# Raw tiles of x landing in the resident array, modulation weights early, loads of two tiles, even shares per step

## The reference, cut to what matters

```python
x = L0_attn_x                                   # (1, 8192, 512)
mod = (_silu(L0_c) @ L0_wmod).reshape(1, 6, 1, 512)
sa, ca, ga, sb, cb, gb = ...                    # ga, gb: magnitude at least 0.25
h = _layernorm(x) * (1 + ca) + sa
x = x + ga * ssm_block(h)     # scan over 8192 steps, 16x16 matrix per channel; layernorm, gelu, W_out, +h
h = _layernorm(x) * (1 + cb) + sb
x = x + gb * ffn_block(h)     # Win, 64 small relu networks of 16, Wout
```

## Time and profile before

| what | us |
|---|---|
| median of 3 runs (lowest, highest) | 761.77 (761.5, 762.27) |
| profiled execution, span of the core from first to last instruction (the only time shown for it) | 763.1 |
| first matmul of the power stage | 10.54 |
| last statistics of x on DVE end | 93.34 |
| last normalised tile on ACT ends | 102.81 |
| first matmul behind the stage (L1185) | 105.20 |

### The profile page before, as it was taken

The page is one execution under the profiler, slowest core; times in us unless marked ns, Lnnn a source line. Parts: engine busy times, 40 slices in busy tenths (PEclk is TensorE's granted clock), DMA queues, the critical chain, the costliest instruction groups (busy, mean ns, idle before and its releaser), DMA issues.

```text
span 763.1 us, 24715 instructions
## 1 busy us (share of the span) xinstructions
PE 706.2 (93%) x10079; PEld 493.9 (65%) x10079; DVE 533.1 (70%) x1192; ACT 470.9 (62%) x1007; POOL 483.1 (63%) x684
## 2 busy tenths in 40 slices
PE   5797978899999898999699999999999999999997
PEld 4774867888899877887545555555455555555564
DVE  7886866844643468544734688788888888877776
ACT  1674966133322471244246888888988888888872
POOL 5664633743455507654288988788888888887710
PEclk9999999999999999999889999999999999999999
DMA  7977400259500002388423002322232232231114
GB/s 223 364 229 274 154 17 3 44 122 174 127 6 4 3 24 45 86 200 177 143 92 111 1 30 82 111 105 81 92 111 83 85 110 84 84 111 55 57 41 153
DMA packets 78209, 78.18 MB, mean 102 GB/s; under 512 B 16144, under 2 KB 49552, under 8 KB 78096
## 3 DMA queue, kind: packets, MB, share of 16 engines
q1 hardware_dynamic: 77072, 74.76, 32.6%
q10 hardware_dynamic: 1024, 1.84, 0.9%
HBM read 59.28 MB, written 17.30 MB: 100 GB/s over the span
## 4 chain that ended last, share of the span: by engine, by line
PE 49%; DVE 1%; POOL 0%; ACT 0%; DVEq 0%; issue 0%; ACTq 0%; POOLq 0%
PE PS L1309 30%; PE PS L1378 4%; PE PS L1356 4%; PE PS L1301 4%; PE PS L1343 4%; PE PS L1393 1%; PE PS L1319 1%; PE PS L1330 0%; ACT arenaC L664 0%; DVE ebs L979 0%; PE PS L1323 0%; DVE arenaC L995 0%; DVEq L86 0%; POOL sy L392 0%; DVE XY L833 0%
## 5 line engine op out<-in xcount | busy, mean ns | idle before, releaser
L1309 PE MATMUL PS<-arenaC,arenaA 128*128 128x512 f32 x512 | 242.0, 605 | 0.0
L408 POOL TENSOR_TENSOR arenaC<-arenaA,par 128x512 f32<-128x512 f32 x104 | 107.3, 1039 | 82.6 <-ACT arenaA L647 41.8
L1309 PEld LDWEIGHTS PS<-arenaC,arenaA 128*128 128x128 f32 x512 | 90.2, 191 | 87.6 <-issue 83.1
L1172 PE MATMUL PS<-arenaA,arenaC 64*64 64x80 f32 (+1 forms) x1792 | 116.4, 233 | 9.0 <-DVE arenaC L821 4.0
L700 ACT ACTIVATE arenaA<-PS,ffc 128x256 f32<-128x256 f32 x224 | 111.8, 578 | 12.3 <-PE PS L1356 12.3
L1175 PE MATMUL PS<-arenaA,arenaC 64*64 64x64 f32 (+1 forms) x1792 | 114.7, 218 | 2.3 <-issue 2.3
L1025 DVE SCALAR_TENSOR_TENSOR PS<-arenaA,ffc,PS 128x256 f32<-128x256 f32 x196 | 95.2, 486 | 22.3 <-ACT arenaA L700 5.7
L1172 PEld LDWEIGHTS PS<-arenaA,arenaC 64*64 64x64 f32 x1792 | 96.0, 138 | 15.6 <-issue 7.9
L821 DVE STREAM_TRANSPOSE arenaC<-arenaC 128x512 f32<-128x512 f32 x104 | 73.0, 705 | 43.1 <-POOL arenaC L408 35.9
L1175 PEld LDWEIGHTS PS<-arenaA,arenaC 64*64 64x64 f32 x1792 | 98.5, 137 | 2.8 <-issue 2.8
L672 ACT ACTIVATE arenaA<-PS,lnwb 128x256 f32<-128x256 f32 x128 | 65.8, 574 | 44.3 <-PE PS L1301 44.3
(11 more groups left out here) (198 smaller groups left out, 1252.3 us busy)
## 6 DMA issues: line engine op xcount, KB each, us to landing
arenaC<-kernel_taps SPq DMA_DIRECT2D x64, 256.0 KB, 4.7
XY<-in_L_attn_x SPq DMA_DIRECT2D x38, 256.0 KB, 5.6
arenaC<-in_L_attn_x SPq DMA_DIRECT2D x15, 512.0 KB, 3.6
out<-arenaC SPq DMA_DIRECT2D x15, 512.0 KB, 2.7
arenaC<-in_L_attn_x SPq DMA_DIRECT2D x26, 256.0 KB, 4.7
XY<-in_L_wmod SPq DMA_DIRECT2D x6, 1024.0 KB, 9.2
XY<-in_L_attn_x SPq DMA_DIRECT2D x11, 512.0 KB, 3.5
out<-XY SPq DMA_DIRECT2D x10, 512.0 KB, 2.8
```

What stands on the lines that cost most here:

```text
L408: gp.tensor_tensor(BDs[:, step % BDR, :, :].rearrange("p g (a m) -> p g a m", m=NS), src, msk, ALU.mult).then_inc(S["bdp_r"], 1)
L1172: pe.matmul(pv_ps(r)[e:e + BW, j, LW - nw:LW + NS], BDTs[e:e + BW, b, j, :], PV[e:e + BW, g, PW - nw:PW + NS], start=True, stop=True)
L1309: mm = pe.matmul(PS[:, 2 + t, :], zT[:, u % 2, q, t * P:(t + 1) * P], WoT[:, q, :], start=False, stop=(q == QB - 1))
```

## The change

**Places for x.** Raw tile c lands in block c//8 + 1 of XY, so one block ahead of where its normalised form goes; the tiles of the last block land in `arenaC` (6) and `UR` (2). No load waits for `xh_r` any more. The weights `wm` take blocks 5, 6 and 7, two each, so that the loads of tiles 32 and 48 wait for `mod_mm` 1 and 2. One DMA loads two tiles, and from tile 4 on one semaphore counts four tiles.

**Order of the weights and steps.** `MOD_AT` puts the six weights after tiles 6, 10, 14, 18, 24 and 30 (pairs); `MOD_A` and `MOD_B` go from steps 12 and 18 to 9 and 15. Both tables of shares are even: 2 or 3 tiles per step, no step with 7.

**Start.** On SP the loads of B and C come first, then A, then `ccol`, then x; the loads of Dm, ln_w and ln_b move to ACT's queue, ahead of the silu. On DVE `first_mix` moves ahead of `crep`, `par` and the other small tables. PE's wait for `crep` and `sel` moves to the step `MOD_A`.

```diff
-XR = 14
 XC = 6
+XL = 2
...
-MOD_A, MOD_B = 12, 18
-MOD_AT = (12, 15, 18, 21, 40, 44)
-STAT_SHARE = [2 if n < 26 else 0 for n in range(28)]
-NORM_SHARE = [2 if n >= 3 else 0 for n in range(28)]
-for step, more in ((12, 5), (13, 1), (18, 4), (21, 1), (25, 1)):
-    STAT_SHARE[step] += more
-for step, more in ((12, 2), (13, 3), (18, 2), (19, 2), (20, 1), (22, 1), (24, 1), (25, 1), (26, 1)):
-    NORM_SHARE[step] += more
+MOD_A, MOD_B = 9, 15
+MOD_AT = (6, 10, 14, 18, 24, 30)
...
+for n, share in enumerate((2, 3, 2, 3, 2, 3, 2, 3, 2, 2, 2, 3, 2, 3, 2, 2, 1, 2, 3, 2, 3, 2, 3, 2, 3, 3, 2, 0)):
+    STAT_SHARE[n] = share
+for n, share in enumerate((0, 0, 2, 2, 2, 2, 3, 3, 3, 1, 2, 3, 2, 2, 3, 3, 1, 2, 2, 3, 2, 3, 2, 3, 2, 3, 4, 4)):
+    NORM_SHARE[n] = share
...
-        wm = [flat_block(5 + min(i // 2, 1))[:, (i % 2) * 2048:(i % 2 + 1) * 2048]...
+        wm = [flat_block(5 + i // 2)[:, (i % 2) * 2048:(i % 2 + 1) * 2048]...
...
+        def raw(c, w=1):
+            b, r = c // CB + 1, c % CB
+            if b < NB:
+                return flat_block(b)[:, r * D:(r + w) * D]
+            return C0[:, 5120 + r * D:5120 + (r + w) * D] if r < XC else UR[:, (r - XC) * D:(r - XC + w) * D]
+
+        def landing(c):
+            return c // XL if c < 2 * XL else 1 + c // (2 * XL)
...
             def load_x(c):
-                if len(users(c)) > 1:
-                    sp.wait_ge(S["xh_r"], users(c)[-2] + 1)
-                sp.dma_start(xst[slot(c)], x_t[:, c, :]).then_inc(x_ld[slot(c)], 16)
+                if c == 4 * CB:
+                    sp.wait_ge(S["mod_mm"], 1)
+                if c == 6 * CB:
+                    sp.wait_ge(S["mod_mm"], 2)
+                sp.dma_start(raw(c, XL)..., x_t[:, c:c + XL, :]).then_inc(x_ld[landing(c)], 16)
...
             def normalise_x(c):
                 act.wait_ge(S["rst_r"], c // LNB + 1)
-                if c % CB == 0 and 5 <= c // CB < 7:
-                    act.wait_ge(S["mod_mm"], c // CB - 4)
-                if c == 4 * CB:
-                    act.wait_ge(S["xh_r"], XR + CB)
-                if c == NC - CB:
-                    act.wait_ge(S["xh_r"], NC - CB)
+                if c % CB == 0 and c:
+                    act.wait_ge(S["xh_r"], c)
```

More of the change, by code:

```diff
@@ L133, in adaln_ssm_kernel @@
         mean_x, rstd_x, nmr_x = (ST[:, i, :] for i in range(3))
-        wm = [flat_block(5 + min(i // 2, 1))[:, (i % 2) * 2048:(i % 2 + 1) * 2048].rearrange("p (k n) -> p k n", k=QB) for i in range(6)]
+        wm = [flat_block(5 + i // 2)[:, (i % 2) * 2048:(i % 2 + 1) * 2048].rearrange("p (k n) -> p k n", k=QB) for i in range(6)]
         crep = GB[:, 0:QB * BR].rearrange("p (k m) -> p k m", k=QB)
@@ L148, in adaln_ssm_kernel, with landed @@
         Tring = [C0[:, c:c + GC * L].rearrange("p (h i) -> p h i", h=GC) for c in (5120, 6144, 7168, 1024, 3072)]
-        xst = [C0[:, 5120 + r * D:5120 + (r + 1) * D] for r in range(XC)]
-        xst += [flat_block(NB - 1)[:, r * D:(r + 1) * D] for r in range(XR - XC)]
-        xst += [UR[:, r * D:(r + 1) * D] for r in range(2)]
-        xst += [flat_block(4)[:, r * D:(r + 1) * D] for r in range(CB)]
-        def slot(c):
-            return XR + c - (NC - 2) if c >= NC - 2 else XR + 2 + c - XR if XR <= c < XR + CB else c % XR
-        def users(c):
-            return [i for i in range(c + 1) if slot(i) == slot(c)]
-        def turn(c):
-            return 16 * len(users(c))
+        def raw(c, w=1):
[5 more added lines that the diff above has]
+            return c // XL if c < 2 * XL else 1 + c // (2 * XL)
+        def landed(c):
+            return 16 if c < 2 * XL else 32
         ktu = C0[:, 6656:6912].rearrange("p (b w) -> p b w", b=2)
@@ L240, in adaln_ssm_kernel @@
         ld_wm = [sem(f"ld_wm{j}") for j in range(6)]
-        x_ld = [sem(f"x_ld{r}") for r in range(len(xst))]
+        x_ld = [sem(f"x_ld{r}") for r in range(landing(NC - 1) + 1)]
         t_ld = [sem(f"t_ld{r}") for r in range(TR)]
@@ L293, in _ @@
                     i = MOD_AT.index(c)
-                    if i >= 4:
-                        sp.wait_ge(S["mod_mm"], 1)
                     j = MOD_ORDER[i]
@@ L538, in _ @@
         def _(act):
+            with nc.allow_non_contiguous_dma(reason="columns of a few hundred elements"):
+                act.dma_start(DmT[:, :], Dm_in.rearrange("(k p) -> p k", p=P)).then_inc(S["ld_small"], 16)
+                act.dma_start(lnwb[:, 0:QB], lnw_in.rearrange("(k p) -> p k", p=P)).then_inc(S["ld_small"], 16)
+                act.dma_start(lnwb[:, QB:], lnb_in.rearrange("(k p) -> p k", p=P)).then_inc(S["ld_small"], 16)
             act.wait_ge(S["ld_c"], 16)
@@ L558, in normalise_x @@
                 act.wait_ge(S["rst_r"], c // LNB + 1)
[L559 to L565 removed]
+                if c % CB == 0 and c:
+                    act.wait_ge(S["xh_r"], c)
+                act.activation(column(c), rows_of(raw(c)), ACT.Identity, scale=rstd_x[:, c:c + 1],
                                bias=nmr_x[:, c:c + 1]).then_inc(S["xh_r"], 1)
@@ L808, in stats_x @@
             def stats_x(c):
-                dve.wait_ge(x_ld[slot(c)], turn(c))
+                dve.wait_ge(x_ld[landing(c)], landed(c))
                 if c >= 4:
                     dve.wait_ge(S["bn_r"], c - 3)
-                chain(dve.bn_stats(bs6[:, c % 4, :], xst[slot(c)]))
+                chain(dve.bn_stats(bs6[:, c % 4, :], raw(c)))
                 dve.bn_aggr(ST[:, 0:2, c], bs6[:, c % 4, :]).then_inc(S["bn_r"], 1)
@@ L871, in last_weights @@
                     dve.wait_ge(S["prep_r"], 2)
-            dve.wait_ge(S["bct_ev"], 1)
+            dve.wait_ge(S["ident_r"], 1)
             first_mix(0)
+            dve.wait_ge(S["silu_r"], 1)
+            dve.tensor_copy(crep, ccol[:, :].unsqueeze(2).to_broadcast([P, QB, BR])).then_inc(S["crep_r"], 1)
+            dve.wait_ge(S["consts"], 3)
+            for e in range(2):
+                dve.reduce_sum(par[:, e:e + 1], mask8[:, e::2], AX.X).then_inc(S["par_r"], 1)
+            for e in range(4):
+                dve.reduce_sum(par4[:, e:e + 1], mask8[:, e::4], AX.X).then_inc(S["par_r"], 1)
+            dve.wait_ge(S["par_r"], 6)
+            dve.reduce_sum(em[:, 0:GC], ident[:, :].rearrange("p (j c) -> p c j", c=GC), AX.X).then_inc(S["em_r"], 1)
+            dve.reduce_sum(em[:, GC:], ident[:, :].rearrange("p (j c) -> p j c", c=GC), AX.X).then_inc(S["em_r"], 1)
+            for i in range(2):
+                dve.tensor_copy(sel[i], ident[:, BR * i:BR * i + 1].to_broadcast([P, P])).then_inc(S["sel_r"], 1)
+            dve.wait_ge(S["em_r"], 2)
+            dve.tensor_copy(spread.rearrange("p (c n) -> p c n", n=NS), em[:, 0:GC].unsqueeze(2).to_broadcast([P, GC, NS])).then_inc(S["pick_r"], 1)
             def column_sums(half, o):
```

45 lines of the change are left out of this document (17 added, 28 removed).

## The result

The changed kernel takes 764.84 us (median of 12 runs, 761.12 to 769.03), the kernel before beside it 761.81 us (12 runs, 759.94 to 766.16): ratio **1.0039 [1.002, 1.0058]**. The change makes the kernel slower by some 0.4%; the forecast was 756.5 us and faster. The profiled execution was the shortest of the 12, 761.12 us with a span of 759.1.

A forecast was written before the change was run, and what follows sets the result against it. Bound: DVE's line to the last tile (93.34 us) and ACT, held up at 68 us, ending at 102.81. DVE 87.3 + 3.3 + 1.8 = 92.4, plus 2.1 + 3.0 = 97.5; 761.77 - 5.3 = 756.5 us, range 753.6 to 760.9.

The forecast's parts named there:

- DVE's line: DVE from first matmul to last statistics: 13.6 start, work, 3.3 of load waits, 1.8 for POOL, ending at 92.4 us.
- The waits for x: DVE's waits for loads of x: 2.1 us at tile 20 and 1.2 at tile 24, 3.3 together.
- those for POOL: DVE's waits for POOL at ends of four-tile groups: six become two, costing 1.8 us.
- The stall's removal: PE's 4.3 us wait for a modulation weight near 68 us goes, and with it ACT's 8.2 us wait and backlog.
- The start: Loads up to PE's first matmul: A lands at 7.9, ccol at 8.5, first matmul at 13.7, 3.2 us later.
- The rivals: Other outcomes: start not late 754.0 us, 0.17; gain eaten 761.6, 0.09; mod_mm late 760.1, 0.05; PE's clock 770, 0.07.
- the loads' for `mod_mm`: Rival: loads of tiles from 32 wait for the modulation product, forecast with 3.5 us to spare; 760.1 us, chance 0.05.
- the clock: Rival: PE at half clock while loads pace it loses 1.7 us per step; 770 us over eight steps, chance 0.07.
- no wait of DVE, PE or ACT over 2.5 us between 45 and 90 us: Sign of being right in the later part of the stage: no longer wait on these three engines.
- the signs of being wrong: Waits for x over 6 us, PE held by a weight, early clock under 0.85, or ACT's backlog past 101 us.
- The end: After DVE's last statistics at 92.4: 2.1 us to the group's factors, 3.0 for ACT's last four normalisings, ending 97.5.
- the check whether ACT can follow: Steps 20 to 27: ACT needs 24.3 us and has 25.3 from 72.2 to 97.5, so it just holds.

The follow-up runs named there:

- e11: The changed kernel with tables altered alone, bursts of 7 statistics tiles at step 9 and 6 at step 15, beside the kernel before: 760.38 us, ratio 0.9985.
- e14: The changed kernel with the bursts of 7 and 6 statistics tiles, run once more beside the kernel before: 760.48 us, ratio 0.9986.
- e8: The kernel before with the change's even tables alone, products left at steps 12 and 18, beside the kernel before: 763.49 us, ratio 1.0035.
- e1: The kernel before, run again with no edit, beside the kernel before: 762.21 us, ratio 1.0013.
- e3: The changed kernel with the old start order of SP, ACT and DVE restored, beside the kernel before: 764.33 us, ratio 1.0035.
- e13: The changed kernel with the old start and bursts of statistics (6 tiles at step 9, 7 at step 15), beside the kernel before: 760.90 us, ratio 0.9992.
- e16: The changed kernel with 6 statistics tiles at steps 9 and 15 and normalising tables laid for ACT, beside the kernel before: 758.92 us, ratio 0.9963.

## Why the prediction was wrong

- **What failed is the step "DVE's line".** It gave 13.6 + 73.7 of work + 3.3 + 1.8 of waits = 92.4. The trace has 82.8 us from 13.9 to 96.7, and 4.1 + 2.4 + 1.6 + 0.9 = 9.0 of waits: 73.8 of work, right to 0.1. The waits for x were 1.6 instead of 3.3, those for POOL 2.4 instead of 1.8. What was not in the sum at all are **5.0 us behind the two modulation products**. The text saw that seven and six tiles had hidden PE's stall from DVE, and put the loss of them in the even tables at nothing. With these 5.0 us the sum gives 97.4, and the trace has 96.6. e11 and e14 (the tables alone altered, with bursts beside the products: 2.3 and 2.1 us are left, and the loss is gone) show that the tables made more than half of them; e8 (even tables on before: 5.2 us of such waits appear) agrees. How much of them is PE's own lateness is not taken apart: the text had the products on PE from 39 to 42.7 us, and they ran from 40.0 to 44.9. But even by its own times the columns would have come a power step of 2.25 us and the column products of 1.05 us later, at about 46 (an estimate), 2 us after DVE stood ready at 43.9. The tail of the tables, which moves the last statistics from step 25 to 26, the text had priced rightly.
- **The base was the later of two ends.** -5.3 was counted from 102.81, ACT's end in one trace, and taken off the median of the runs. The other traces of before have 98.86 and 102.62. The forecast 97.5 was only 1.4 us below before's early end. Also the span was read as the runs' time, "1.3 us over the median": a run's time is 1.7 to 1.8 us more than its span in every run of e1, so that execution was some 3 us over. The mean of before's three last tiles is 101.4, so 1.4 us under the base that was taken.
- **The stall's removal came true, its worth did not.** ACT is busy between 68 and 77 us, PE waits for no weight, and though `mod_mm` came 2.2 us later than forecast (44.9), DVE waited for no tile behind it. The last tile came at 102.2 all the same, as DVE's last statistics were 3 to 7 us later than in the three traces of before.
- **The start was right by two errors.** 13.7 forecast, 13.99 measured. A landed at 6.5 (7.9 forecast) and `ccol` at 7.1 (8.5): beside three column loads A took 4.5 us from issue, 0.4 more than before, not 1.9. By the rule cited from the Trainium skill (DMA: Bandwidth & Descriptors, Queues, rings and completion order), that engines take turns between queues, some delay was due; the trace agrees with the sharing and shows it to be small. Against that, from the end of `mix` to the first matmul it took 5.7 us instead of 3.8: moving `first_mix` ahead put the small tables behind it, onto this path and beside POOL's work (last section), and the text gave that no price. The later start was then costed in full, but the stream of loads covers it (e3, e13).
- **The rivals.** None of them was it. The wait that took the place of the one removed was DVE's for the product, not the loads' for `mod_mm`; the clock stayed at 1.00 in the stage of this trace. Of what the text wanted to see, "no wait of DVE, PE or ACT over 2.5 us between 45 and 90 us" did not come (DVE's wait of 4.1 us ended at 48.05, one of ACT's of 2.6 us at 66.8), the silu was early (7.1) and the last normalising late (99.1 to 102.2); of the signs of being wrong, the stage's end after 101 us did.
- **The end** was 5.5 us after the last statistics against 5.1: right. In the check whether ACT can follow, 72.2 needs seven transposes; with the six that the text names it is 72.8, and nothing hangs on it.
- **What stays open.** The change is 3 us slower by the medians, while its stage ends 1.6 us later in the mean of three traces (105.4 against 103.8). Three traces each, with before's spread of 4 us, can't resolve that; 0.3 us lie outside the span (time less span 2.0 to 2.1 in the change's profiled runs, 1.7 to 1.8 in before's).

## What to carry to other kernels

A lumpy share of work per step may be cover for something long on another engine: before evening it out, ask of each lump what runs beside it, and price that at its full length. Moving a load earlier moves what waits behind it and what computes on it too; here the place of the weights forced early products, and only tables made for those steps (e16) turned the loss of 0.4% into a gain of 0.4%, part of which lies behind the stage. And take the base from several traces where a wait hangs on a load.
